# Latent cross attention from a transposed context: norm folded into the weights, f32r key projection, new order of rounds

## What is computed

```python
def layernorm(x, g, b):
    mu = jnp.mean(x, axis=-1, keepdims=True)
    var = jnp.mean((x - mu) ** 2, axis=-1, keepdims=True)
    return (x - mu) * jax.lax.rsqrt(var + LN_EPS) * g + b
def rmsnorm(x, gamma):
    norm = jnp.sqrt(jnp.sum(x * x, axis=-1, keepdims=True)) * x.shape[-1] ** (-0.5)
    return x / jnp.maximum(norm, RMS_EPS) * gamma
xn = layernorm(x, ln_x_g, ln_x_b)            # context, 32 x 1601 x 192
ln = layernorm(latents, ln_l_g, ln_l_b)      # latents, 32 x 64 x 256
q = ln @ Wq.T
kv = jnp.concatenate([xn @ Wkv.T, ln @ Wlkv.T], axis=1)
k, v = (kv[..., :INNER], kv[..., INNER:])    # INNER = 256, 4 heads of 64
qn = rmsnorm(q, qn_g) * SCALE
kn = rmsnorm(k, kn_g)
attn = softmax(where(mask, qn @ kn.T, -max)) # over 1601 context keys and 64 latent keys
out = (attn @ v) @ Wo.T + bo
```

## Time and profile before

| what | us |
|---|---|
| median of 3 runs (4118.66 to 4123.49) | 4119.8 |
| the profiled execution | 4116.67 |
| its span in the trace | 4114.9 |
| TensorE matmul busy (80% of the span) | 3302.6 |
| VectorE busy (64%) | 2630.0 |
| ScalarE busy (46%) | 1901.4 |
| GpSimd busy (8%) | 315.2 |

### The profile page before, as it was taken

How to read it: one execution, slowest core, us unless ns; L and a number is a source line. 1 busy time by engine, 2 the same in 40 slices (tenths; PEclk the granted TensorE clock), 3 DMA queues, 4 the chain that set the end, 5 groups by cost and what they waited for, 6 DMA issues and landing times. The chain is left out here.

```text
span 4114.9 us, 98818 instructions
## 1 busy us (share of the span) xinstructions
PE 3302.6 (80%) x34538; PEld 2870.1 (70%) x34538; DVE 2630.0 (64%) x8299; ACT 1901.4 (46%) x3959; POOL 315.2 (8%) x323
## 2 busy tenths in 40 slices
PE   3489999999999999454446999999999999844484
PEld 3378888888888888333335888888888888733353
DVE  5477777777777775466666777777677777465000
ACT  1145555555545544132233666666566666522110
POOL 0200000000000000000002111111111111000101
PEclk7689999999989999676677999999999999965687
DMA  2111111111111110200001111111111111120611
GB/s 63 59 34 38 38 42 40 39 42 40 39 38 41 37 40 17 67 21 20 10 13 51 40 39 40 39 39 40 37 41 40 39 40 39 37 67 31 212 57 59
DMA packets 206338, 181.54 MB, mean 44 GB/s; under 512 B 65260, under 2 KB 199457, under 8 KB 205728
## 3 DMA queue, kind: packets, MB, share of 16 engines
q1 hardware_dynamic: 203808, 168.59, 14.1%
q0 software_dynamic: 2048, 6.68, 0.5%
HBM read 146.95 MB, written 28.39 MB: 43 GB/s over the span
## 5 line engine op out<-in xcount | busy, mean ns | idle before, releaser
L1768 DVE CUSTOM_DVE_ANT_0 xb_junk<-xb_ring,xb_mbias 128x372 bf16<-128x372 f32 (+2 forms) x1024 | 544.5, 572 | 174.8 <-PE xb_ring L1676 153.1
L1607 ACT ACTIVATE xb_P<-xb_sc 124x1024 f32<-124x1024 f32 (+1 forms) x416 | 426.0, 1026 | 376.0 <-PE xb_sc L1700 374.1
L704 PE MATMUL xa_ring<-xa_wf,xa_xT 96*124 96x256 f32 (+1 forms) x1664 | 401.2, 392 | 15.9 <-DVE xa_xT L818 12.3
L704 PEld LDWEIGHTS xa_ring<-xa_wf,xa_xT 96*124 96x124 f32 (+1 forms) x1664 | 315.2, 193 | 75.5 <-issue 22.1
L679 PE MATMUL xa_acc<-xa_xhat,xa_P 124*128 124x193 f32 x1664 | 314.1, 330 | 0.0
L1647 PE MATMUL xb_ring<-xb_xst,xb_whi 128*128 128x372 f32 (+2 forms) x768 | 262.5, 369 | 38.7 <-DVE xb_xst L1747 32.8
L1676 PE MATMUL xb_ring<-xb_khi,xb_qhi 64*128 64x372 f32 (+2 forms) x1024 | 266.4, 401 | 26.7 <-DVE xb_klo L1753 16.9
L1647 PE MATMUL xb_ring<-xb_whi,xb_xst 128*124 128x256 f32 (+1 forms) x1248 | 285.1, 291 | 2.5
L1700 PE MATMUL xb_sc<-xb_qhi,xb_khi 64*124 64x256 f32 (+1 forms) x1664 | 282.1, 372 | 0.0
L1753 DVE TENSOR_TENSOR xb_klo<-xb_ring,xb_khi 128x372 fp32r<-128x372 f32 (+2 forms) x256 | 138.6, 571 | 210.2 <-ACT xb_khi L1573 209.2
L679 PEld LDWEIGHTS xa_acc<-xa_xhat,xa_P 124*128 124x128 f32 x1664 | 267.2, 190 | 5.5 <-issue 5.5
(11 more groups left out here) (391 smaller groups left out, 7479.2 us busy)
## 6 DMA issues: line engine op xcount, KB each, us to landing
xa_raw<-in_ctx SPq DMA_DIRECT2D x64, 279.0 KB
ex_w<-in_W SPq DMA_DIRECT2D x16, 1024.0 KB, 8.7
xa_raw<-in_ctx SPq DMA_DIRECT2D x32, 372.0 KB
xb_raw<-in_ctxT SPq DMA_DIRECT2D x64, 186.0 KB
xb_raw<-in_ctxT SPq DMA_DIRECT2D x32, 248.0 KB
xa_mask<-in_mask SPq DMA_DIRECT2D x32, 200.1 KB
xb_mask<-in_mask SPq DMA_DIRECT2D x32, 200.1 KB
xa_raw<-in_ctx SPq DMA_DIRECT2D x32, 186.0 KB
```

The costliest lines, as they stand in the source:

```text
L704: i = nc.tensor.matmul(bank[0:KEYS, 256 * (t % 2):256 * (t % 2) + 256], xT[0:H + h, c % 2, h, t * KEYS:(t + 1) * KEYS], wf[0:H + h, h, 0:256],
L1607: nc.scalar.activation(P[0:w, pbuf(c, p), :], sc[(c + p) % 2][0:w, :], ACT.Exp).then_inc(sem("exped"), 1)
L1768: v.tensor_tensor_reduce(out=junk[:, k, 0:w], in0=ring[f % 3][:, 0:w], in1=mbias[:, p, k0:k0 + w], scale=1.0, scalar=-3.0e38, op0=ALU.add, ...
```

## The change

The norm is no longer applied to the context. The mean is taken out of the weights (each column of `wf` loses its mean over the 192 inputs, since the RMS norm that follows the keys is blind to their length), the bias is added as sigma times the bias row, and the weighing takes the raw tokens with `1/sigma` put into the exponential as a bias of ScalarE's (`nlr`). The keys are projected from a second copy of the context that arrives already transposed (`ctxT`, which a later stage uses too), so the transposes of `xhat` go. The projection is done in f32r with the operands split in a high part and a rest: five matmuls of 256 columns a tile for two in fp32. Sigma itself is transposed by TensorE (kind ST, one transpose a tile) and copied by ScalarE (SE). GpSimd makes the high parts of the last 64 input rows (kind X) and rounds the keys (`kTr`), which ScalarE did. The context and the small tensors are held three deep, so loads of batch n+3 start when batch n is weighed. PSUM banks: F1, F2, AL and M now go through the ring too. The list of rounds is new, F1 and F2 of a batch stand in the round after it, and the loop runs 12 rounds a turn, two turns, where it ran 10 and three.

```diff
-    STEADY = 10
+    STEADY = 12
+    DEEP = 3
-        ROUNDS = [("T", 0), ("X1", 1), ("M", 0), ("K", 0), ("B", 0), ("X2", 1), ("X1", 2), ("R1", 0), ("T", 1),
...
-                  ("PVend", 0), ("R2", 3), ("A", 2), ("KT", 3), ("F0", 0), ("F1", 0), ("A", 3), ("AL", 0),
-                  ("mred", 0), ("F2", 0)]
+        ROUNDS = [("K", 1), ("Q", 0), ("B", 0), ("R", 0), ("X", 3), ("RS", 1),
+                  ("B", 1), ("PV", 0), ("KT", 0), ("R", 1), ("ST", 3), ("K", 2), ("SE", 3), ("Yn", 0), ("RS", 2),
+                  ("B", 2), ("PV", 1), ("A", 0), ("YAn", 0), ("KT", 1), ("R", 2), ("YBn", 0),
+                  ("B", 3), ("PV", 2), ("F1", 0), ("A", 1), ("STn", 0), ("Xn", 0), ("K", 3), ("SEn", 0), ("Yn", 1), ("RS", 3),
+                  ("B", 4), ("PV", 3), ("YAn", 1), ("KT", 2), ("R", 3), ("YBn", 1), ("F2", 0), ("Yn", 2),
+                  ("B", 5), ("PV", 4), ("YAn", 2), ("A", 2), ("STn", 1), ("Xn", 1), ("KT", 3), ("SEn", 1), ("YBn", 2), ("Yn", 3),
+                  ("B", 6), ("PV", 5), ("A", 3), ("AL", 0), ("STn", 2), ("Xn", 2), ("mred", 0), ("YAn", 3), ("SEn", 2), ("YBn", 3),
+                  ("Kn", 0), ("RSn", 0), ("PV", 6), ("M", 0), ("F0", 0)]
-                if kind == "T" and c == 0:
+                if kind == "Q":
...
+                    nc.gpsimd.tensor_scalar(augk[64:65, p, 0:PAD], mask8[64:65, t, :], -1.0, -MASKED, ALU.add, ALU.mult).then_inc(sem("augk"), 1)
+                if kind == "X":
...
+                    nc.gpsimd.tensor_copy(xhl[0:64, k0:k0 + W], xTr[0:64, 1, k0:k0 + W])
+                    nc.gpsimd.tensor_copy(xhs[0:64, k0:k0 + W], xTr[0:64, 1, k0:k0 + W]).then_inc(sem("xhi2"), 1)
+                if kind == "KT":
...
+                    nc.gpsimd.tensor_copy(kTr[:, c % 2, :, 0:W], kT[:, p, :, k0:k0 + W]).then_inc(sem("kTr"), 1)
+                if kind == "YA":
+                    nc.scalar.activation(lnv[0:KEYS, t0:t0 + nt], moments[0:KEYS, t0:t0 + nt, 1], ACT.Ln, bias=eps[0:KEYS]).then_inc(sem("ln"), 1)
...
+                    nc.scalar.activation(raw[0:KEYS, t, t0:t0 + nt, DC], lnv[0:KEYS, t0:t0 + nt], ACT.Exp, scale=0.5).then_inc(sem("sigma"), 1)
...
+                if kind == "X":
...
+                    nc.scalar.activation(xh[:, k0:k0 + W], xTr[:, 0, k0:k0 + W], ACT.Copy).then_inc(sem("xhi"), 1)
-                        nc.scalar.activation(kTr[:, h, 0:W], ring[f % len(ring)][:, 0:W], ACT.Copy).then_inc(sem("kT_out"), 1)
-                        nc.scalar.activation(P[0:KEYS, c % 2, :], s[0:KEYS, :], ACT.Exp).then_inc(sem("exped"), 1)
+                    nc.scalar.activation(P[0:KEYS, b_, 0:256], s_[0:KEYS, 0:256], ACT.Exp, bias=nlr[0:KEYS, t, 2 * c:2 * c + 1])
-                            i = nc.tensor.transpose(bank[0:hi, t * KEYS:(t + 1) * KEYS],
-                                                    xhat[0:KEYS, p, t0 + t, H * h:H * h + hi], ident[0:KEYS, 0:KEYS])
+                        i = nc.tensor.transpose(bank[0:96, t * KEYS:(t + 1) * KEYS], sig[0:KEYS, t0 + t, :].bitcast(F32), ident[0:KEYS, 0:KEYS])
-                                i = nc.tensor.matmul(bank[0:KEYS, 256 * (t % 2):256 * (t % 2) + 256],
-                                                     xT[0:H + h, c % 2, h, t * KEYS:(t + 1) * KEYS], wf[0:H + h, h, 0:256],
+                            nc.tensor.matmul(o, xh[:, keys], wh[:], start=True, stop=False)
+                            nc.tensor.matmul(o, xh[:, keys], wl[:], start=False, stop=False)
+                            nc.tensor.matmul(o, xhl[:, keys], whh[:], start=False, stop=False)
+                            nc.tensor.matmul(o, xl[:, keys], wh[:], start=False, stop=False)
+                            i = nc.tensor.matmul(o, xhs[:, keys], wls[:], start=False, stop=True)
-                        i = v.tensor_scalar(xhat[0:KEYS, p, t, 0:DC], raw[0:KEYS, t, :], moments[0:KEYS, t, 0:1],
-                                            rstd[0:KEYS, t:t + 1], ALU.subtract, ALU.mult)
-                    v.tensor_copy(xT[:, c % 2, 1, 0:W], ring[f % len(ring)][0:H + 1, 0:W]).then_inc(sem("xT1"), 1)
+                if kind == "YB":
...
+                    v.tensor_scalar(nlr[0:KEYS, t3, t0:t0 + nt], lnv[0:KEYS, t0:t0 + nt], -0.5, None, ALU.mult)
+                    v.tensor_tensor(sig[0:KEYS, t0:t0 + nt, 65], raw[0:KEYS, t3, t0:t0 + nt, DC], sig[0:KEYS, t0:t0 + nt, 64].bitcast(F32),
+                                    ALU.subtract).then_inc(sem("siglo"), 1)
+                if kind == "X":
...
+                    v.tensor_tensor(xl[:, cols], xTr[:, 0, cols], xh[:, cols].bitcast(F32), ALU.subtract)
+                    v.tensor_tensor(xhl[64:128, cols], xTr[0:64, 1, cols], xhl[0:64, cols].bitcast(F32), ALU.subtract).then_inc(sem("xlo"), 1)
-                        v.tensor_copy(augk[64:65, p, 0:PAD], mbias[64:65, p, :]).then_inc(sem("augk"), 1)
-                    chain.step(v.tensor_copy(augq[0:33, :], sc[0][0:33, 0:256]))
-                    v.tensor_tensor(augq[32:33, :], sc[0][32:33, 0:256], augq[32:33, :], ALU.subtract).then_inc(sem("augq"), 1)
```

526 lines of the change are left out of this document (312 added, 214 removed), and 3 rows, old and new, of the table ROUNDS.

## The result

The changed kernel takes 3949.2 us (median of 4 runs, 3947.3 to 3953.0) against 4119.2 for the kernel before (4 runs, 4113.8 to 4123.5): a ratio of 0.9589, 95% interval 0.9572 to 0.9606. It was faster, as forecast; 3,910 was forecast and 3,949 came, inside the range. The profiled execution took 3947.3 us, its span 3945.2.

A forecast was written before the change was run, and what follows sets the result against it. TensorE was taken to bound the kernel, VectorE next. Rounds of 37.8 us (33.9 work, 3.9 waits) with start and end saved 205 us, 4116.7 to 3912, median 3915; predicted 3,910, range 3,825 to 4,005.

The forecast's parts named there:

- TensorE's own work: TensorE's busy time per round: 39.0 less 5.1 from cheaper K, transposes and M, giving 33.9 us.
- The port: GpSimd's port shared with VectorE: of 11.2 us GpSimd work a round, some 4 us reach VectorE's queue.
- the 15 us of the two kinds: VectorE work a round of the kinds GpSimd holds up: khat, X, Newton steps, YB, mred and others, some 15 us.
- The queue of 35.4 us: VectorE's queue a round: 31.4 us plus some 4 of port delay, above TensorE's 33.9, so both wait for each other.
- the three waits: TensorE's waits at KT of chunk 0, ST of chunk 0 and KT of chunk 3: together 3.9 us, port about half.
- The waits: TensorE waits 1.5 us at KT of chunk 0, 1.5 at ST of chunk 0, 0.9 at KT of chunk 3.
- The round of 37.8 us: Time from F0 to F0: TensorE's 33.9 us of work plus 3.9 us of waits.
- The clock: TensorE's clock in the rounds: full, since waits are short and apart, none as long as the old 2.2 us.
- The rival on the other side: Slower than before: clock low for long every round, TensorE waiting at all three places; 4,215 us at 20 us low; chance 0.04.
- I take the first M at 249: Start of the kernel: first M at 249 us instead of 245.4, memsets growing about 11 us against a shorter first key chain.
- The upper bound of +12: Start of the kernel: the most by which the first M was expected to come later; after 257 counted as wrong.
- the worst case of 42.6 us a round: Port rule at its hardest: all 11.2 us of GpSimd's work fall on VectorE, 42.6 us a round, some 4,060 us in all.

The follow-up runs named there:

- e5_k4: Changed kernel without one of the five matmuls of K (context times the weights' low part): 3923.1 us, round 37.1 us.
- e4_pool_small: Changed kernel with GpSimd's X, keys and two masks cut to 8 columns, leaving out needed work: 3871.8 us, round 35.6 us.
- e6_f1_end: Changed kernel with F1 put back at the end of its own round, behind F0: 4154.2 us, 1.0089 of the kernel before.
- e11_order2: Changed kernel with e8_start2's start and a second order of rounds (factor of chunk 0 first, statistics of chunks 2 and 3 behind maxima): 3908.6 us.
- e12_order2_keys: e11_order2 with the keys rounded by ScalarE instead of GpSimd: 3946.7 us, round 39.0 to 39.5 us.
- e1_memset: Changed kernel with three GpSimd memsets shrunk to what no load writes: 3936.9 us, first F0 at 301.3 us.
- e8_start2: e2_start with the loads of batch 2 issued behind the transposed context of batch 1: 3924.4 us, first F0 at 287.5 us.
- e3_keys_act: Changed kernel with the keys rounded by ScalarE instead of GpSimd: 3982.9 us, round 39.0 to 39.4 us.
- e2_start: e1_memset with the weights' round trip issued behind chunk 0's loads and their low parts made behind chunk 0's statistics: 3944.9 us.

## Why the prediction was right, and where it was off

**TensorE's own work: right.** 33.9 us were forecast and 34.1 came: the pitch of 0.12, the 13 transposes of ST and the two of M are as priced.

**The port: right as a mechanism, wrong in its places.** Half of 11.2 us with slack, some 4, was forecast for VectorE's queue; 3.1 came, in the instructions that are short, not in khat and the subtractions that the prediction counted among the 15 us of the two kinds. Without it VectorE is busy 28.0, forecast 29.2. The queue of 35.4 us, longer than TensorE's 33.9, from which the prediction concluded that the two wait for each other, did not come: it is 32.8 with its small gaps, and 5.1 us of the round are idle. The waits come from where the steps stand and not from a full queue. That the port makes about half of the three waits was right in the sum, 2.0 of 3.7, but not at KT of chunk 0, where the prediction saw GpSimd beside the chain and 0.2 of 1.2 went.

**The waits: right.** 1.5, 1.5 and 0.9 were forecast, 1.17, 1.36 and 0.90 came, and 0.21 at K. The round of 37.8 us is 37.9. The places were reasoned out and held; that the sum lies within 0.1 us is in part luck, with the two errors above in it. The two engines wait for each other: e5_k4 shows that half of a saving on TensorE is lost, and e4_pool_small that a saving on GpSimd alone, for which TensorE never waits, is worth 2.3 us a round.

**The clock: right, and worth more than the step said.** The prediction put full clock down to short and separate waits, and it stayed at 1.00. The move of F1 decides it: e6_f1_end undoes that alone and loses 7.0 us a round, 205 us in all, more than the 170 that the whole change brings. In this order of rounds the cheaper K and T would not have shortened the kernel with F1 at its old place. How much the old kernel would gain from the move of F1 alone was not run. The rival on the other side (the clock low for long in every round) was priced for low clock at all three waits; e6_f1_end ends on its side with low stretches at two, 224 us of them between the first F0 and the last. What was not foreseen is that the fall is no matter of one wait's length: 2.2 us had it in 29 of 30 rounds of the kernel before, 2.6 in 8 of 21 in e11_order2 and 28 of 29 in e12_order2_keys, 1.8 in 26 of 29 in e6_f1_end and in one of 29 in the changed kernel.

**The step that failed: "I take the first M at 249".** It came at 271.7. The prediction took the memsets' growth as about 11 us, which is what it was (first load at 183.87 for 172.88), and as mostly covered by a shorter first key chain. It missed two things. The scaling of the weights waits for the memsets, and the weights' round trip stood on SyncE behind all loads of batch 0, with VectorE's first statistics behind that again. e1_memset gives back 11.5 us, e8_start2 another 13.8. The upper bound of +12 was thus too low as well. The other 13 us are 3.6 in the rounds and the loop's turns, 5.5 behind the last F0 in later stages, whose cause was not sought, and what the predicted number was set below its own sum (3,910 for 3,915), less about 1 by which the median lies nearer to the profiled execution than was assumed. The total fell inside the range in spite of this step because the range was 180 us wide.

The Trainium skill's rule (SBUF — State Buffer, Who interferes with whom) was named for the worst case of 42.6 us a round, every GpSimd microsecond on VectorE. The rows do not bear that sum out: 3.1 of 11 us fell on VectorE. They do bear out its rule that the holder keeps the port for the whole instruction: L972 above, 1.53 us for 0.17.

## What to carry to other kernels

Before pricing the instructions of a round, find the waits beside which the clock falls: one step moved by half a round was worth 7.0 us a round here, the cheaper K 3.5 by the pitches. Count in how many rounds a fall stands beside a wait, and do not go by its length. When GpSimd shares work with VectorE, look at which VectorE instruction stands at the head of the queue when each GpSimd one starts; long GpSimd instructions belong beside VectorE's sums, statistics and maxima, not beside a chain of small steps for which others wait. When work is taken off GpSimd, look at where the rest of its queue moves: e3_keys_act took the keys' copies off it, 3.5 us a round, and lost 1.1 to 1.5. Where a result falls into a rival's range, look in the trace for the rival's wait before it is called the cause. And follow the first batch through the queue of DMA issues: what the second batch needs first must not stand behind what the third needs.

## What was not expected of the hardware

A memset of GpSimd, which only writes, holds a VectorE scalar operation: 96x512 elements took 11.06 us beside memsets of 6.37, 2.78, 4.13 and 0.73 us. In the kernel before, with GpSimd idle, the same takes 0.47:

```profile
187.23 0.47 DVE L783 TENSOR_SCALAR xa_wf<-xa_w_raw,xa_gcol 96x512 f32<-96x512 f32 x1
```

It started at 172.09, inside the first, and ended at 183.15; the four memsets end at 175.40, 178.13, 182.20 and 182.87, and a fifth starts at 182.82, so it got in behind none of the first three. In the rounds a held instruction mostly ended behind one GpSimd copy.

Issuing DMAs on SyncE takes long where many are queued: the loads of batches 1 and 2, 20 issues, took 38 us in e2_start, single ones between 0.42 and 4.05. Each chunk's load waits for the same chunk of the batch before, but these waits cost nothing here: the issues follow each other from 205.93 to 243.89 us with no gap of 0.1 us, so the time is spent in the issues themselves. Why they are long was not tested.
